# Cross attention: reciprocals in two halves over two steps, quotients in a third, output product two steps later

## Chip, cores and metric

The kernel runs on one core of a Trainium2 chip. The metric is the device time of one execution in microseconds (us); the median of three runs stands for a kernel.

## What is computed

The reference is a chain of six blocks on x (32 x 64 x 256): cross attention to ctx (32 x 1601 x 128), self attention, a layer of experts, a second cross attention to the same ctx, a state space block in two directions, and a feed forward block. The change is in the code of the cross attention, which the kernel calls twice (tags x0 and x1; the profile prints both as x). Cut to what matters:

```python
qh = (q @ Wq + bq).reshape(B, LQ, HEADS, D_K)      # q: layer norm of x, 32 x 64 x 256
kh = (k @ Wk + bk).reshape(B, LKV, HEADS, D_K)     # k = v = ctx, LKV = 1601, 16 heads of 16
vh = (v @ Wv + bv).reshape(B, LKV, HEADS, D_K)
scores = einsum('bhqd,bhkd->bhqk', qh, kh) * scale
attn = softmax(scores, axis=-1)
out = einsum('bhqk,bhkd->bhqd', attn, vh)
x = x + concat(out) @ Wo + bo
```

## The kernel before

One image (index b or u, 32 of them) is worked off in NG = 7 steps g = 0 to 6, each with two tiles of 128 keys (the last step has one, of 65). The loop over all steps s = 7u + g is unrolled, and each engine has its own list in program order; they meet at semaphores. In step s of image u there are:

- TensorE: `largest` (M, four products, L481: scores of image u + 1 for their maxima; two quads of heads ahead of the scores, two inside them), `scores` (L557, and L563, which subtracts the maximum), `project_keys` (K, L468: a seventh of a later image's keys), `project_values` (V, L499), in step 6 `turn_maxes` (T, L489: transposes of the negated maxima), then `weigh` (P, L531: probabilities times values of the step before). Step 1 adds `spread_sums` (S, L507), which spreads the softmax sums of the image before over the rows. `project_out` (W, L514) is the output product of two finished images, once in two images.
- VectorE: `keep_max` (L714, four reductions that read M), `keep_shift` in step 6 (L721 and L724), `gather` (L748 and L751: adds P's result to u_sb), `keep_sums` (L728) in step 1, `divide` (L733 reciprocal of the sums, L735 quotients oT = u_sb times reciprocal) and `add_out` (L740: adds W's result to x).
- ScalarE: the exponentials (L654), and copies of K and V out of their banks (L627, L635). GpSimd: kT_hi (L678), the queries (L663) and the split of the raw context into two parts (L367, L369). The queue of SP loads the raw context.

K's seven shares go over six stretches of 512 keys and a narrow one of 65 keys for both halves of the features; `key_share` hands the narrow share to K in step 4, and the maxima of the narrow share are M of step 6.

What ties the engines: M, K, V, T, P, S and W all write into misc_ps, a ring of NMB = 4 PSUM banks in the order of the list ORDER. An operation waits until the operation four places before it in ORDER has been read out (`open_bank`), by ScalarE for K and V and by VectorE for all others. The counts are worked out from the same list `step_ops`, so moving an operation there moves its place in the ring.

Around the change, VectorE in image u > 0 does in step 2: four maxima, `divide` of image u - 1 (both instructions), `gather`. In step 3 of even images TensorE ends the step with W, and VectorE with `add_out`. In the last image (u = 31) there are no maxima, K or V left, and after the loop the last S, divide and W stand alone.

Of the kernel before, what the change touches and what calls it, by code (L numbers as in the profile page):

```python
# [14 lines left out]
B, LQ, D = 32, 64, 256  # L15
# [246 lines left out]
def cross_attention(nc, tag, x_sb, ident, x_sel, pair_mask, ctxT, wq, wk, wv, wo, bq, bv, bo):  # L262
# [3 lines left out]
    GROUPS = 4  # L266
# [22 lines left out]
    def key_share(u, g):  # L289

        return (u + 1 + (g + 2) // NG, (g + 2) % NG)
# [4 lines left out]
    def step_ops(s):  # L296

        u, g = divmod(s, NG)
        ops = [("M", u + 1, g, j) for j in TRAIL + LEAD] if u + 1 < B else []
        if key_share(u, g)[0] < B:  # L300
            ops.append(("K",) + key_share(u, g))
        if s + 2 < STEPS:
            ops.append(("V", s + 2))
        if g == NG - 1 and u + 1 < B:
            ops.append(("T", u + 1))
        if s > 0:
            ops.append(("P", s - 1))
        if g == 1 and u > 0:
            ops.append(("S", u - 1))
        if g == 3 and u % 2 == 0 and u > 0:  # L310
            ops.append(("W", u // 2 - 1))
        return ops

# [9 lines left out]
    with ExitStack() as ctx:  # L323
# [77 lines left out]
        sums = sb(f"{tag}_sums", [P, GROUPS * LQ])  # L401
        recip = sb(f"{tag}_recip", [P, GROUPS * LQ])
# [15 lines left out]
        recip_done = sem(f"{tag}_recip_done")  # L418
# [14 lines left out]
        def read_out(e, op):  # L433

            reader, n = READ[AT[op]]
            e.wait_ge(act_free if reader == "act" else dve_free, n)
# [10 lines left out]
        def _(pe):  # L447
# [13 lines left out]
            def project_keys(op):  # L461
                _, b, n = op
                dst = open_bank(op)
                pe.wait_ge(raw_lo_done, split_of(b, SHARES[n][0][1]))
                for m, (c, k0, kn) in enumerate(SHARES[n]):
                    kn += kn % 2
                    for i, (w, part) in enumerate(((wk_hi, raw_hi), (wk_lo, raw_hi), (wk_hi, raw_lo))):
                        ins = nc.tensor.matmul(dst[:, m * kn:(m + 1) * kn], w[:, c * P:(c + 1) * P],  # L468
                                               part[:, b % 2, k0:k0 + kn], start=i == 0, stop=i == 2)
                ins.then_inc(misc_ready, 1)  # L470
# [14 lines left out]
            def turn_maxes(op):  # L485
                dst = open_bank(op)
                pe.wait_ge(max_done, op[1] + 1)
                for c in range(KD):
                    ins = nc.tensor.transpose(dst[:, c * P:(c + 1) * P],  # L489
                                              neg_max[:, c, :, :].rearrange("p j n -> p (j n)"), ident[:, :])  # L490
                ins.then_inc(misc_ready, 1)

            def project_values(op):
                b, g = divmod(op[1], NG)
                dst = open_bank(op)
                pe.wait_ge(raw_lo_done, split_of(b, tiles(g)[-1] * P))
                for h, i in enumerate(tiles(g)):
                    for m, (part, w) in enumerate(((raw_hi, wv_hi), (raw_hi, wv_lo), (raw_lo, wv_hi))):
                        ins = nc.tensor.matmul(dst[0:keys(i), h * D:(h + 1) * D], part[:, b % 2, cols(i)], w[:, :],  # L499
                                               start=m == 0, stop=m == 2)  # L500
                ins.then_inc(misc_ready, 1)
# [98 lines left out]
            for s in range(STEPS):  # L600
                u, g = divmod(s, NG)
                scores(s)
                if key_share(u, g)[0] < B:
                    project_keys(("K",) + key_share(u, g))
                if s + 2 < STEPS:
                    project_values(("V", s + 2))
                if g == NG - 1 and u + 1 < B:
                    turn_maxes(("T", u + 1))
                if s > 0:
                    weigh(("P", s - 1))  # L610
                if g == 1 and u > 0:
                    spread_sums(("S", u - 1))
                if g == 3 and u % 2 == 0 and u > 0:
                    project_out(("W", u // 2 - 1))
            weigh(("P", STEPS - 1))
            spread_sums(("S", B - 1))
# [89 lines left out]
        @block.vector  # L706
        def _(dve):
            def keep_max(op):
                _, b, n, j = op
                made(dve, op)  # L710
                c, k0, kn = SHARES[n][0]
                m = len(SHARES[n])
                even = kn + kn % 2
                nc.vector.tensor_reduce(maxes[:, c:c + m, j, k0 // NB],  # L714
                                        bank(op)[:, 0:m * even].rearrange("p (c k) -> p c k", c=m)[:, :, 0:kn],
                                        AX.X, ALU.max).then_inc(dve_free, 1)

            def keep_shift(op):
                b = op[1]
                read_out(dve, ORDER[max(n for n in range(AT[op]) if ORDER[n][0] == "M")])  # L720
                nc.vector.tensor_reduce(neg_max[:, :, :, 0], maxes[:, :, :, :], AX.X, ALU.max, negate=True  # L721
                                        ).then_inc(max_done, 1)
                made(dve, op)
                nc.vector.tensor_copy(shift[:, b % 2, :], bank(op)[:, 0:2 * P]).then_inc(dve_free, 1)  # L724

            def keep_sums(op):
                made(dve, op)
                nc.vector.tensor_copy(sums[:, :], bank(op)[:, 0:GROUPS * LQ]).then_inc(dve_free, 1)  # L728

            def divide(op):  # L730
                b = op[1]
                read_out(dve, op)
                nc.vector.reciprocal(recip[:, :], sums[:, :]).then_inc(recip_done, 1)  # L733
                dve.wait_ge(recip_done, b + 1)
                nc.vector.tensor_tensor(oT[:, :, b % 2, :], u_sb[:, b % 2, :, :],  # L735
                                        recip[:, :].rearrange("p (r q) -> p r q", q=LQ), ALU.mult).then_inc(o_done, 1)

            def add_out(op):
                made(dve, op)
                nc.vector.tensor_tensor(x_sb[:, op[1], :], bank(op)[:, 0:D], x_sb[:, op[1], :], ALU.add).then_inc(dve_free, 1)  # L740

            def gather(op):

                b, g = divmod(op[1], NG)
                total = u_sb[:, b % 2, :, :].rearrange("p r q -> p (r q)")
                made(dve, op)
                if g == 0:
                    nc.vector.tensor_copy(total, bank(op)[:, 0:GROUPS * LQ]).then_inc(dve_free, 1)  # L748
                else:
                    read_out(dve, ("P", op[1] - 1))  # L750
                    nc.vector.tensor_tensor(total, bank(op)[:, 0:GROUPS * LQ], total, ALU.add).then_inc(dve_free, 1)  # L751

            nc.vector.memset(ones[:, :].bitcast(F32), 1.0)
            nc.vector.memset(neg_max[:, :, :, :], 0.0)
            nc.vector.memset(oT[:, :, :, :], 0.0).then_inc(const_done, 1)
            dve.wait_ge(const_done, 1)
            if bo is not None:
                made(dve, ("C",))
                nc.vector.tensor_tensor(bias[:, :], bank(("C",))[:, 0:D], bo_sb[:, :], ALU.add).then_inc(dve_free, 1)
                read_out(dve, ("C",))  # L760
                nc.vector.tensor_tensor(x_sb, x_sb, bias[:, :].rearrange("p (a d) -> p a d", a=1).broadcast_to([P, NT, D]),
                                        ALU.add).then_inc(bias_done, 1)
                dve.wait_ge(bias_done, 1)
            for n in range(NG):
                for j in range(QUADS):
                    keep_max(("M", 0, n, j))
            keep_shift(("T", 0))
            for s in range(STEPS):
                u, g = divmod(s, NG)
                if u + 1 < B:  # L770
                    for j in TRAIL + LEAD:
                        keep_max(("M", u + 1, g, j))
                if g == 2 and u > 0:
                    divide(("S", u - 1))
                if g == NG - 1 and u + 1 < B:
                    keep_shift(("T", u + 1))
                if s > 0:
                    gather(("P", s - 1))
                if g == 1 and u > 0:
                    keep_sums(("S", u - 1))  # L780
                if g == 3 and u % 2 == 0 and u > 0:
                    add_out(("W", u // 2 - 1))
            gather(("P", STEPS - 1))
            keep_sums(("S", B - 1))
            divide(("S", B - 1))
            add_out(("W", B // 2 - 1))

# [1434 lines left out]
```

## Time and profile before

| | |
|---|---|
| median of three runs | 4064.31 us (4061.2 to 4066.16) |
| the profiled execution | 4061.75 us |
| its span on the core | 4059.8 us |
| first cross attention, main loop | about 92 to 1054 us of the span |
| second cross attention, main loop | about 1843 to 2790 us |
| TensorE busy | 3550.4 us, 87% |
| VectorE busy | 2756.5 us, 68% |
| ScalarE busy | 1951.2 us, 48% |
| GpSimd busy | 1562.0 us, 38% |

PE is TensorE, PEld its weight loads (which run beside the products), DVE VectorE, ACT ScalarE, POOL GpSimd. A row of a timeline gives the start and the duration in us, engine, line, operation, the tile written and the tiles read, the shape and the number of instructions merged; in brackets stands how long the engine had been idle before it, and what ended that. Ends of TensorE's products are modelled. The profile is of one execution; all durations below are from it.

### The profile page before, as it was taken

What the parts mean: (1) busy time and instruction counts of PE and PEld (TensorE: products, weight loads), DVE (VectorE), ACT (ScalarE), POOL (GpSimd) and SP (SyncE); (2) the same over time, 40 slices, a digit from 0 to 9 for tenths busy, and PEclk for the clock granted to TensorE, in tenths of its full rate; (3) what the DMA queues carried; (4) which work ended last, traced back from release to release, by engine and by line L of the source; (5) the groups of instructions that cost most, each with busy time, mean ns of one, the idle gap of its engine ahead of it and who ended that gap; (6) DMA issues with size and microseconds to landing.
All of it is one profiled execution on the core that took longest, in us unless ns stands there. A gap on an engine that the chain in (4) does not pass through costs nothing. (4 is left out here: it accounts for less than half of the span.)

```text
span 4059.8 us, 128360 instructions
## 1 busy us (share of the span) xinstructions
PE 3550.4 (87%) x53914; PEld 2521.8 (62%) x53915; DVE 2756.5 (68%) x4627; ACT 1951.2 (48%) x3015; POOL 1562.0 (38%) x1491
## 2 busy tenths in 40 slices
PE   6999999999783699669999999998788888877778
PEld 4888888888672466448888888885233333333357
DVE  5777777777543122257777777776799999999964
ACT  2666666666441122126666666664444444444432
POOL 3333333333132100233333333330088777778800
PEclk8999999999895899869999999998898989999889
DMA  2010010000006100110100010000132222222200
GB/s 67 28 36 28 28 34 29 28 28 20 10 1 244 46 31 31 49 56 28 36 28 28 30 33 28 28 20 25 24 81 71 72 70 68 70 72 81 72 25 21
DMA packets 79948, 182.69 MB, mean 45 GB/s; under 512 B 10754, under 2 KB 31266, under 8 KB 79042
## 3 DMA queue, kind: packets, MB, share of 16 engines
q1 hardware_dynamic: 76354, 166.57, 13.2%
q8 instruction: 421, 6.90, 0.7%
q0 software_dynamic: 3072, 8.39, 0.6%
q14 instruction: 101, 0.83, 0.1%
HBM read 157.36 MB, written 17.56 MB: 43 GB/s over the span
## 5 line engine op out<-in xcount | busy, mean ns | idle before, releaser
L654 ACT ACTIVATE x_probs<-x_score_ps 128x1024 f32<-128x1024 f32 (+1 forms) x896 | 814.2, 960 | 708.2 <-PE x_score_ps L563 701.9
L714 DVE TENSOR_REDUCE x_maxes<-x_misc_ps 128x1 f32<-128x512 f32 (+1 forms) x1792 | 1020.9, 625 | 31.0 <-PE x_misc_ps L481 25.6
L678 POOL CAST x_kT_hi<-x_kT 128x512 fp32r<-128x512 f32 (+1 forms) x448 | 256.3, 572 | 1286.5 <-ACT x_kT L627 1063.1
L1742 PE MATMUL b_acc_ps<-b_read,ident 128*128 128x512 f32 x1024 | 571.1, 689 | 183.5 <-POOL b_read L1828 150.3
L1820 POOL TENSOR_TENSOR b_drive<-b_b_all,b_dtx 128x1024 f32<-128x1024 f32 x256 | 602.6, 2355 | 332.8 <-DVE b_dtx L1900 282.0
L1862 DVE TENSOR_TENSOR_SCAN b_state<-b_decay_ps,b_drive 128x512 f32<-128x512 f32 x512 | 607.0, 1205 | 12.5 <-POOL b_drive L1820 12.5
L557 PE MATMUL x_score_ps<-x_qz,x_kT 32*128 32x128 f32 x13312 | 591.2, 277 | 1.4 <-issue 1.2
L1810 ACT ACTIVATE b_decay_ps<-b_dt,b_a_neg 128x504 f32<-128x504 f32 x512 | 350.0, 685 | 462.3 <-DVE b_state L1862 462.3
L1742 PEld LDWEIGHTS b_acc_ps<-b_read,ident 128*128 128x128 f32 x1024 | 196.1, 213 | 503.8 <-POOL b_read L1828 251.1
L557 PEld LDWEIGHTS x_score_ps<-x_qz,x_kT 32*128 32x128 f32 x13312 | 501.4, 182 | 4.5 <-issue 2.5
L531 PE MATMUL x_misc_ps<-x_probs,x_v 128*32 128x64 f32 x26624 | 464.5, 221 | 0.0
L481 PE MATMUL x_misc_ps<-x_kT_hi,x_qz_hi 32*128 32x512 f32 (+1 forms) x2048 | 451.0, 410 | 11.8 <-POOL x_kT_hi L678 3.0
L531 PEld LDWEIGHTS x_misc_ps<-x_probs,x_v 128*32 128x32 f32 x26624 | 392.2, 110 | 65.7 <-issue 23.2
L751 DVE TENSOR_TENSOR x_u<-x_misc_ps,x_u 128x256 f32<-128x256 f32 x384 | 162.1, 422 | 324.0 <-PE x_misc_ps L531 324.0
L563 PE MATMUL x_score_ps<-x_shift,x_ones 1*128 1x512 f32 (+1 forms) x1792 | 327.5, 458 | 1.2 <-issue 1.1
L627 ACT ACTIVATE x_kT<-x_misc_ps 128x512 f32<-128x512 f32 (+1 forms) x448 | 250.2, 558 | 86.7 <-PE x_misc_ps L468 86.7
L481 PEld LDWEIGHTS x_misc_ps<-x_kT_hi,x_qz_hi 32*128 32x128 f32 x2048 | 219.6, 186 | 114.0 <-DVE x_u L751 31.2
L635 ACT ACTIVATE x_v<-x_misc_ps 128x512 f32<-128x512 f32 (+1 forms) x448 | 259.2, 578 | 24.0 <-PE x_misc_ps L499 11.8
L1872 DVE TENSOR_TENSOR b_read<-b_c_ps,b_state 128x512 f32<-128x512 f32 x384 | 254.0, 662 | 0.3 <-DVE b_state L1862 0.3
L468 PE MATMUL x_misc_ps<-x_raw_hi,x_wk_hi 128*128 128x512 f32 (+1 forms) x512 | 232.9, 455 | 15.8 <-POOL x_v L684 8.9
L369 POOL TENSOR_TENSOR x_raw_lo<-x_raw,x_raw_hi 128x512 fp32r<-128x512 f32 (+1 forms) x192 | 235.7, 1228 | 15.6
L499 PE MATMUL x_misc_ps<-x_wv_hi,x_raw_hi 128*128 128x256 f32 (+1 forms) x832 | 237.8, 286 | 0.0
(283 smaller groups left out, 5607.9 us busy)
## 6 DMA issues: line engine op xcount, KB each, us to landing
x_raw<-in_ctxT SPq DMA_DIRECT2D x64, 800.5 KB, 4.5
b_b_all<-b_bc_rows SPq DMA_DIRECT2D x128, 256.0 KB, 3.6
b_c_all<-b_bc_rows SPq DMA_DIRECT2D x128, 256.0 KB, 3.1
m_w<-in_m_w SPq DMA_DIRECT2D x16, 704.0 KB, 19.3
m_w<-in_m_w SPq DMA_DIRECT2D x8, 768.0 KB, 20.3
m_slot_rows<-m_zero SPq DMA_DIRECT2D x1, 4992.0 KB, 17.2
m_block_rows<-m_slot_rows SPq DMA_DIRECT2D x39, 128.0 KB, 2.0
m_slot_out<-m_out SPq DMA_DIRECT2D x39, 128.0 KB, 1.7
```

The lines of the kernel that those rows point to most:

```text
L481: ins = nc.tensor.matmul(dst[:, m * kn:(m + 1) * kn], qz_hi[rows, b % 2, c, :, :].rearrange("p s q -> p (s q)"), kT_hi[rows, (b * NG + n) ...
L531: ins = nc.tensor.matmul(dst[j * 32:(j + 1) * 32, r * LQ:(r + 1) * LQ], v_sb[0:keys(i), g, h, 8 * c + 2 * j + half, :], probs[0:keys(i), s ...
L557: nc.tensor.matmul(score_ps[0:kn, j, n * P:(n + 1) * P], kT[rows, u % 2, c, cols(mine[h])], qz[rows, u % 2, c, :, :].rearrange("p s q -> p ...
L563: nc.tensor.matmul(score_ps[0:kn, j, 0:len(mine) * 2 * P], ones[j * 32:j * 32 + 1, 0:kn], shift[j * 32:j * 32 + 1, u % 2, :].rearrange("p ...
L635: nc.scalar.activation(v_sb[rows, g, 0:n, :, 0:DH].rearrange("p a h d -> p (a h) d"), bank(op)[rows, 0:n * D].rearrange("p (a d) -> p a d" ...
L654: nc.scalar.activation(probs[rows, s % 2, js, 0:n], score_ps[rows, js, 0:n], ACT.Exp).then_inc(exp_done, 1)
L678: nc.gpsimd.tensor_copy(kT_hi[:, at % 3, 0:m * even].rearrange("p (c k) -> p c k", c=m)[:, :, 0:kn], kT[:, b % 2, c:c + m, k0:k0 + kn]).th ...
L714: nc.vector.tensor_reduce(maxes[:, c:c + m, j, k0 // NB], bank(op)[:, 0:m * even].rearrange("p (c k) -> p c k", c=m)[:, :, 0:kn], AX.X, AL ...
L1742: nc.tensor.matmul(acc_ps[:, c, :], ident[:, :], read[:, c, :], start=False, stop=True, skip_group_check=True).then_inc(acc_done, 1)
L1810: nc.scalar.activation(by_sequence(decay_ps[:, c % 2, :])[:, :, inside(p)], by_sequence(dt[:, c, :])[:, :, inside(p)], ACT.Exp, scale=a_ne ...
L1820: nc.gpsimd.tensor_tensor(drive[:, c:c + 2, :], b_all[:, k % 2:k % 2 + 1, :].broadcast_to([P, 2, NB]), dtx[:, c:c + 2, :], ALU.mult).then_ ...
L1862: nc.vector.tensor_tensor_scan(order(state[:, c, :]), order(decay_ps[:, c % 2, :]), order(drive[:, c, :]), 0.0, ALU.mult, ALU.add).then_in ...
```

## The change

`divide` becomes two functions. `invert(op, half)` takes the reciprocal of 128 of the 256 columns of the sums; it runs in step 2 for the first half and in step 3 for the second. `divide` now only makes the quotients, in step 4. `project_out` and `add_out` move from step 3 to step 5 of even images, in `step_ops`, in TensorE's loop and in VectorE's. Behind the loop both halves, the quotients and the last W follow each other as before.

```diff
--- before.py
+++ after.py
@@ -307,7 +307,7 @@
             ops.append(("P", s - 1))
         if g == 1 and u > 0:
             ops.append(("S", u - 1))
-        if g == 3 and u % 2 == 0 and u > 0:
+        if g == 5 and u % 2 == 0 and u > 0:
             ops.append(("W", u // 2 - 1))
         return ops
 
@@ -610,7 +610,7 @@
                     weigh(("P", s - 1))
                 if g == 1 and u > 0:
                     spread_sums(("S", u - 1))
-                if g == 3 and u % 2 == 0 and u > 0:
+                if g == 5 and u % 2 == 0 and u > 0:
                     project_out(("W", u // 2 - 1))
             weigh(("P", STEPS - 1))
             spread_sums(("S", B - 1))
@@ -727,11 +727,16 @@
                 made(dve, op)
                 nc.vector.tensor_copy(sums[:, :], bank(op)[:, 0:GROUPS * LQ]).then_inc(dve_free, 1)
 
+            HALF = GROUPS * LQ // 2
+
+            def invert(op, half):
+                read_out(dve, op)
+                of = slice(half * HALF, (half + 1) * HALF)
+                nc.vector.reciprocal(recip[:, of], sums[:, of]).then_inc(recip_done, 1)
+
             def divide(op):
                 b = op[1]
-                read_out(dve, op)
-                nc.vector.reciprocal(recip[:, :], sums[:, :]).then_inc(recip_done, 1)
-                dve.wait_ge(recip_done, b + 1)
+                dve.wait_ge(recip_done, 2 * b + 2)
                 nc.vector.tensor_tensor(oT[:, :, b % 2, :], u_sb[:, b % 2, :, :],
                                         recip[:, :].rearrange("p (r q) -> p r q", q=LQ), ALU.mult).then_inc(o_done, 1)
 
@@ -770,7 +775,9 @@
                 if u + 1 < B:
                     for j in TRAIL + LEAD:
                         keep_max(("M", u + 1, g, j))
-                if g == 2 and u > 0:
+                if g in (2, 3) and u > 0:
+                    invert(("S", u - 1), g - 2)
+                if g == 4 and u > 0:
                     divide(("S", u - 1))
                 if g == NG - 1 and u + 1 < B:
                     keep_shift(("T", u + 1))
@@ -778,10 +785,12 @@
                     gather(("P", s - 1))
                 if g == 1 and u > 0:
                     keep_sums(("S", u - 1))
-                if g == 3 and u % 2 == 0 and u > 0:
+                if g == 5 and u % 2 == 0 and u > 0:
                     add_out(("W", u // 2 - 1))
             gather(("P", STEPS - 1))
             keep_sums(("S", B - 1))
+            for half in range(2):
+                invert(("S", B - 1), half)
             divide(("S", B - 1))
             add_out(("W", B // 2 - 1))
```

VectorE's list, from the copy of the sums in step 1 of an even image to the maxima of step 4. Before (L728 the sums, L714 four maxima, L733 reciprocal, L735 quotients, L751 gather, L740 add_out):

```order
L728 COPY x_sums<-x_misc_ps 128x256
L714 TENSOR_REDUCE x_maxes<-x_misc_ps 128x1 x4
L733 RECIPROCAL x_recip<-x_sums 128x256
L735 TENSOR_TENSOR x_oT<-x_u,x_recip 128x4x64
L751 TENSOR_TENSOR x_u<-x_misc_ps,x_u 128x256
L714 TENSOR_REDUCE x_maxes<-x_misc_ps 128x1 x4
L751 TENSOR_TENSOR x_u<-x_misc_ps,x_u 128x256
L740 TENSOR_TENSOR x<-x_misc_ps,x 128x256
L714 TENSOR_REDUCE x_maxes<-x_misc_ps 128x1 x4
```

The same stretch now, on to step 6 (L735 is now the reciprocal, L740 the quotients, L756 the gather, L745 add_out):

```order
L728 COPY x_sums<-x_misc_ps 128x256
L714 TENSOR_REDUCE x_maxes<-x_misc_ps 128x1 x4
L735 RECIPROCAL x_recip<-x_sums 128x128
L756 TENSOR_TENSOR x_u<-x_misc_ps,x_u 128x256
L714 TENSOR_REDUCE x_maxes<-x_misc_ps 128x1 x4
L735 RECIPROCAL x_recip<-x_sums 128x128
L756 TENSOR_TENSOR x_u<-x_misc_ps,x_u 128x256
L714 TENSOR_REDUCE x_maxes<-x_misc_ps 128x1 x4
L740 TENSOR_TENSOR x_oT<-x_u,x_recip 128x4x64
L756 TENSOR_TENSOR x_u<-x_misc_ps,x_u 128x256
L714 TENSOR_REDUCE x_maxes<-x_misc_ps 128x1 x4
L756 TENSOR_TENSOR x_u<-x_misc_ps,x_u 128x256
```

Between the maxima and the gather of step 2 stood two instructions of full width; now one of half width stands there in step 2, one in step 3, and the quotients in step 4.

TensorE's list at the first place where W moves, the difference of the two (L531 the value products, L514 W, L481 the maxima of the next step, narrow in the second piece):

```order
@@ -359,5 +359,4 @@
 L499 MATMUL x0_misc_ps<-x0_wv_hi,x0_raw_lo 128x256
 L531 MATMUL x0_misc_ps<-x0_probs,x0_v 32x64 x32
-L514 MATMUL x0_misc_ps<-x0_wo,x0_oT 128x256 x4
 L481 MATMUL x0_misc_ps<-x0_kT_hi,x0_qz_hi 128x512 x2
 L557 MATMUL x0_score_ps<-x0_qz,x0_kT 128x128 x14
@@ -392,4 +391,5 @@
 L499 MATMUL x0_misc_ps<-x0_wv_hi,x0_raw_lo 128x256
 L531 MATMUL x0_misc_ps<-x0_probs,x0_v 32x64 x32
+L514 MATMUL x0_misc_ps<-x0_wo,x0_oT 128x256 x4
 L481 MATMUL x0_misc_ps<-x0_kT_hi,x0_qz_hi 128x66 x4
 L557 MATMUL x0_score_ps<-x0_qz,x0_kT 65x128 x6
```

W stood between step 3 and the wide step 4; it stands now between step 5 and the narrow step 6.

## Rows read from the trace of the kernel before

**Rows 1.** The page, busy us of each engine, share of the span, instructions.

```profile
PE 3550.4 (87%) x53914; PEld 2521.8 (62%) x53915; DVE 2756.5 (68%) x4627; ACT 1951.2 (48%) x3015; POOL 1562.0 (38%) x1491
```

**Rows 2.** Busy time in a stretch: length, PE, PEld, DVE, ACT, POOL, TensorE's granted clock, DMA share, GB/s.

```profile
200.00:500.00 300.00, 296.93 (x7317) 246.12 (x7306) 216.22 (x393) 187.18 (x273) 100.97 (x144) 1.00 0.10 31
```

**Rows 3.** Who waited for whom, 100 to 1060 us: us in total, times, longest.

```profile
...
PEld x_misc_ps L468 <- DVE x_maxes L714: 16.9, 48, 0.4
PEld x_misc_ps L481 <- DVE x_u L751: 15.7, 29, 0.6
...
```

**Rows 4.** Timeline of TensorE, steps 2 to 4 of an odd image.

```profile
...
496.24 1.10 PE L531 MATMUL x_misc_ps<-x_probs,x_v 128*32 128x64 f32 x64
...
499.61 0.50 PE L468 MATMUL x_misc_ps<-x_raw_hi,x_wk_hi 128*128 128x512 f32 x1
...
501.20 1.10 PE L531 MATMUL x_misc_ps<-x_probs,x_v 128*32 128x64 f32 x64
...
503.79 0.30 PE L468 MATMUL x_misc_ps<-x_raw_hi,x_wk_hi 128*128 128x66 f32 x1
...
```

**Rows 5.** Timeline of VectorE, the same steps.

```profile
...
493.60 2.48 DVE L714 TENSOR_REDUCE x_maxes<-x_misc_ps 128x1 f32<-128x512 f32 x4
496.00 1.74 DVE L733 RECIPROCAL x_recip<-x_sums 128x256 f32<-128x256 f32 x1
497.78 0.84 DVE L735 TENSOR_TENSOR x_oT<-x_u,x_recip 128x256 f32<-128x256 f32 x1
498.54 0.41 DVE L751 TENSOR_TENSOR x_u<-x_misc_ps,x_u 128x256 f32<-128x256 f32 x1
...
502.37 0.42 DVE L751 TENSOR_TENSOR x_u<-x_misc_ps,x_u 128x256 f32<-128x256 f32 x1 [1.03 <-PE x_misc_ps L531]
502.77 2.48 DVE L714 TENSOR_REDUCE x_maxes<-x_misc_ps 128x1 f32<-128x512 f32 x4
506.13 0.42 DVE L751 TENSOR_TENSOR x_u<-x_misc_ps,x_u 128x256 f32<-128x256 f32 x1 [0.87 <-PE x_misc_ps L531]
...
```

**Rows 6.** Timelines of TensorE and VectorE, steps 3 to 6 of an even image.

```profile
...
532.05 1.99 PE L514 MATMUL x_misc_ps<-x_wo,x_oT 128*128 128x256 f32 x8
...
536.70 1.10 PE L531 MATMUL x_misc_ps<-x_probs,x_v 128*32 128x64 f32 x64
...
540.90 1.10 PE L531 MATMUL x_misc_ps<-x_probs,x_v 128*32 128x64 f32 x64
...
544.40 0.38 PE L489 MATMUL x_misc_ps<-ident,x_neg_max 128*128 128x128 f32 x2
...
```

```profile
...
534.08 0.42 DVE L740 TENSOR_TENSOR x<-x_misc_ps,x 128x256 f32<-128x256 f32 x1 [1.47 <-PE x_misc_ps L514]
...
542.07 0.42 DVE L751 TENSOR_TENSOR x_u<-x_misc_ps,x_u 128x256 f32<-128x256 f32 x1 [1.32 <-PE x_misc_ps L531]
...
543.42 0.19 DVE L721 TENSOR_REDUCE x_neg_max<-x_maxes 128x8 f32<-128x32 f32 x1
544.82 0.42 DVE L724 CAST x_shift<-x_misc_ps 128x256 fp32r<-128x256 f32 x1 [1.21 <-PE x_misc_ps L489]
...
```

**Rows 7.** Timelines of TensorE and VectorE, steps 2 and 3 of image u = 30.

```profile
...
1018.72 1.10 PE L531 MATMUL x_misc_ps<-x_probs,x_v 128*32 128x64 f32 x64
...
1020.29 0.42 DVE L735 TENSOR_TENSOR x_oT<-x_u,x_recip 128x256 f32<-128x256 f32 x1
...
1023.29 1.10 PE L531 MATMUL x_misc_ps<-x_probs,x_v 128*32 128x64 f32 x64
...
```

**Rows 8.** Groups by line: total busy us, mean ns of one, idle before.

```profile
...
L733 DVE RECIPROCAL x_recip<-x_sums 128x256 f32<-128x256 f32 x64 | 111.5, 1742 | 0.1
...
L1021 DVE RECIPROCAL s_recip<-s_sums 128x16 f32<-128x16 f32 x16 | 4.0, 253 | 0.6
...
```

**Rows 9.** Timeline of GpSimd, steps 2 to 4 of the odd image of rows 4.

```profile
...
497.72 0.61 POOL L663 TENSOR_TENSOR x_qz_hi<-x_qT,x_mask 128x256 fp32r<-128x256 f32 x1
...
506.00 0.29 POOL L678 CAST x_kT_hi<-x_kT 128x130 fp32r<-128x130 f32 x1 [2.30 <-ACT x_kT L627]
...
```

## The prediction

> **What bounds the kernel now.** I read the page's busy row first: TensorE is busy 87% of the span, VectorE 68%, ScalarE 48% [rows 1]. The busy time by stretch sharpens this for the code in question: in 300 us inside the first attention TensorE works 297 us at the full granted clock (1.00, that is 2.4 GHz), VectorE 216 us [rows 2]. So an attention lasts as long as TensorE's list of work, plus the few places where TensorE stops. A shorter VectorE list is worth nothing by itself; only what removes a stop of TensorE counts.
>
> The view of who waited for whom gives the stops [rows 3]. In the first attention TensorE's loads sit idle 29 times, 15.7 us in all, before the maxima's matmuls (L481) until VectorE's gather (L751), and 16.9 us before the key projection (L468) until a maximum (L714). 29 is nearly the number of images in which VectorE divides while the next image's maxima are computed: u = 1 to 30. So once an image something on VectorE is late.
>
> The timelines show it [rows 4, 5]. In the image at 490 us, step g = 2 ends with the value products (L531) at 496.24 + 1.10 = 497.34. The gather that empties their bank should follow 0.07 us later, as it does in the next step (502.30, gather at 502.37). It starts at 498.54, since VectorE has done four maxima (to 496.08), then the reciprocal (1.74) and the quotients (0.84). In the next step the second leading maximum needs that bank: banks go round in fours. It, the first maximum behind the gather and then the keys wait in turn: the key projection starts at 499.61. Two distances follow.
> - Undisturbed, the keys start 1.49 us after the products' end (503.79 - 502.30).
> - After a late gather they start 1.07 us after its start (499.61 - 498.54).
>
> So a gather may start 0.42 us behind the products' end and cost nothing. Beyond that TensorE pays all of it: 498.54 + 1.07 - 497.34 - 1.49 = 0.78 us. The interval between the products' starts says the same: 501.20 - 496.24 = 4.96 in step 3, against 540.90 - 536.70 = 4.20 in step 5, which has the same tiles and no divide [rows 4, 6]. I take 0.77.
>
> A check comes with the trace. The quotients take 0.84 us in most images, but 0.42 in u = 30. There the interval is 1023.29 - 1018.72 = 4.57, and the stop 0.37: 0.41 less for 0.42 us less on VectorE [rows 7]. The cost is one to one.
>
> **What the change does to this stop.** The reciprocal of 128x256 takes 1742 ns, that of 128x16 elsewhere in the kernel 253 ns [rows 8]. That is (1742 - 253)/240 = 6.2 ns a column, and 253 + 112 x 6.2 = 947 ns for 128x128. Two halves take 1.89 us, 0.15 more than the whole. Bounds for a half: 0.87 (no fixed part) and 1.74 (width has no effect); the line between two measured widths lies close to the first. Now step by step, with what hides each piece.
> - Step 2: the maxima end at 496.08 and the gather is due at 497.41, a gap of 1.33 us. A half with 0.04 us of gap before the next instruction ends at 497.07. Slack 0.34, and another 0.35 before TensorE notices. The stop of 0.77 goes.
> - Step 3: the gather now starts at 497.41, four maxima end 0.40 + 2.48 later at 500.29, and the products, undisturbed, end at 497.34 + 4.20 = 501.54. The second half ends at 501.28, 0.33 before the gather's turn at 501.61.
> - Step 4: the narrow key share makes this the short one. The maxima end at 505.25 and the gather is due at 506.13: 0.88 us [rows 5]. The quotients fit if they take 0.84 and with room at 0.42. If they were late by 0.1, step 5 is a wide step and forgives 0.35. Cost 0.
> - What is late next: after that no step of the image has VectorE work besides its own. TensorE then runs step 3 like step 5, which shows that neither ScalarE nor GpSimd nor a DMA holds a wide step above 4.20. The raw context tiles come on SP's queue, which is moved past nothing.
>
> How long will the quotients be? GpSimd's row says why they take 0.84: in step 2 its products for qz_hi start at 497.72 and run 0.61 us, under the quotients at 497.78. In u = 30 there is no such product beside them, and they take 0.42. In step 4 GpSimd sits idle for 2.30 us up to 506.00, just when the quotients run (505.3 to 505.7) [rows 5, 7, 9]. So I take 0.42. The Trainium skill has the rule (SBUF — State Buffer, "Who interferes with whom"): a VectorE instruction with two SBUF inputs contends with a GpSimd instruction that reads SBUF, and the later one waits. The trace agrees here, with 0.84 beside such a product and 0.42 without it. By that rule the quotients shrink; by the flat reading they stay at 0.84; both fit the gap, so the sum is the same.
>
> The output product W (four products in eight passes, 1.99 us) moves from behind step 3 to behind step 5 of every even image, 30 times inside the loop. Its price on TensorE stays, since it waits for quotients that are a whole step old. New is what stands behind it: step 6, the narrow one, where fewer scores stand ahead of the second leading maximum, so that it asks sooner for the bank that add_out empties. add_out starts 0.04 us after W's end (534.08 against 534.04) and takes 0.42 [rows 6]. The gather does the same job for the narrow step today: starts at 542.07, 0.07 after the products' end, takes 0.42, and no row of the waits puts a stop of the narrow step on it: the 29 are the divides. add_out is even 0.03 nearer to its products' end. So I put W's cost there at 0; as its bound I allow a tenth of a us, 30 x 0.1 = 3 us, inside the range.
>
> Behind W on VectorE stand add_out, four narrow maxima (542.49 to 543.42: 0.93) and the negated maximum of all (0.19), and the transposes T need these. Today T starts at 544.40, 0.79 us after the negated maximum is done at 543.61; the distance to the step's start stays the same with W ahead. Cost 0.
>
> Last image: there are no maxima, nothing waits, and reciprocal, quotients and W stand in a row at the end of each attention. Two halves cost 2 x 0.15 = 0.3 us more.
>
> Sum: 58 images x 0.77 = 44.7, two images (u = 30) x 0.37 = 0.7, less 0.3 for the tails: 45.1 us saved. The profiled execution took 4061.75 us (span 4059.8), 2.6 below the median of 4064.31. I take the gain off the median: 4064.3 - 45.1 = 4019.2; off the profiled run it is 4016.7.
>
> **Rivals.**
> 1. Only part comes back (4026 to 4045). Something makes the gather late by more than 0.42 us again, in step 2, 3 or 4. A half would have to take over 0.95 + 0.34 + 0.35 = 1.64 us for that, so only the upper bound (1.74) would do it, and then by 0.1. Or a wait that today lies under the stop shows, say 0.3 us of ScalarE or GpSimd in 60 steps: 18 us, 4037. For it speaks that the step's key projection waits for a maximum 48 times, more often than there are divides [rows 3]; against it that step 5 has the same tiles and takes 4.20.
> 2. It does not do what it says (4060 to 4068): the stop belongs to the maxima's matmuls or to ScalarE, and the reciprocal only lies beside it. The image u = 30, where less VectorE time gave less stop one to one, speaks against it.
> 3. Slower, by W ahead of the narrow step. The mechanism: add_out, four narrow maxima, the negated maximum and the copy of T's result (0.42 + 0.93 + 0.19 + 0.42 = 1.96 us) stand behind W on VectorE. If none of it were covered, 30 x 1.96 = 59 us are lost against 45 won: 4078. It decides from 45/30 = 1.5 us a W. Against it: 0.79 us of slack before T and an even spacing today.
> 4. VectorE's list as the bound, with the fixed part of a reciprocal paid twice. If the attention were as long as that list, 62 x 0.15 = 9.3 us would come on top: 4074, less what shorter quotients give back. It decides only where VectorE has no idle time in a step; it is busy for 216 of 300 us [rows 2], so it is not so. The Trainium skill speaks against small pieces (VectorE: DVE Perf Modes, the section on the TRN2 errata): each instruction pays a latency of its own, so a large tile is better than many small ones. The trace agrees that there is a fixed part.
>
> **How the numbers follow.** The forecast, all of the stop gone, has 0.84; rival 1 has 0.08, rival 2 0.03, rivals 3 and 4 together 0.03, and a gain above the forecast's range 0.02. The forecast's own scatter: single runs of before differ by 5 us (4061.2 to 4066.2), and a new build may lay its instructions otherwise; I allow 7 us to either side. That makes 4012 to 4027; to bring in rival 1's near half I extend the upper end to 4031. A measurement here tells 0.2% (8 us) from no change; so faster 0.95, same 0.02, slower 0.03.
>
> **What would show it.** In the profile after: the L481 row waiting for the gather and the L468 row waiting for maxima (15.7 and 16.9 us) shrink, the first to near nothing; the interval from step 2's to step 3's products goes from 4.96 to 4.20; the halves take 0.95; the quotients 0.42; W's row stays at 1.99, with no new wait of L481 for add_out. Wrong would be: an interval in step 3 above 4.3, a late gather in step 4, or T starting later after W. A half above 1.64 us would bring the stop back.

## The result

| | before | changed |
|---|---|---|
| median | 4063.06 us (4 runs, 4061.2 to 4066.16) | 4011.8 us (4 runs, 4010.0 to 4014.43) |
| span of the profiled execution | 4059.8 us | 4008.4 us |

The ratio is 0.9874, 95% interval [0.9856, 0.9891]: 51 us or 1.3% faster. Forecast were 4019 us and a gain of 45 us, between 4012 and 4031. The time lies 0.2 us below that range, and the gain is 6 us larger than forecast. A second comparison of the same two kernels, made with the experiments, gave 4013.2 us for the changed one, inside the range.

TensorE's timeline in an odd image of the changed kernel, steps 2 to 4, answers to [rows 4]:

```profile
...
485.59 1.10 PE L531 MATMUL x_misc_ps<-x_probs,x_v 128*32 128x64 f32 x64
...
488.19 0.50 PE L468 MATMUL x_misc_ps<-x_raw_hi,x_wk_hi 128*128 128x512 f32 x1
...
489.78 1.10 PE L531 MATMUL x_misc_ps<-x_probs,x_v 128*32 128x64 f32 x64
...
493.55 1.10 PE L531 MATMUL x_misc_ps<-x_probs,x_v 128*32 128x64 f32 x64
...
```

The products of step 3 start 489.78 - 485.59 = 4.19 us after those of step 2; it was 4.96. The keys start 488.19 - 486.69 = 1.50 us after the products' end, undisturbed.

VectorE's timeline in the same image answers to [rows 5] (L735 is the reciprocal, L740 the quotients, L756 the gather):

```profile
...
482.99 2.48 DVE L714 TENSOR_REDUCE x_maxes<-x_misc_ps 128x1 f32<-128x512 f32 x4
485.39 0.94 DVE L735 RECIPROCAL x_recip<-x_sums 128x128 f32<-128x128 f32 x1
486.76 0.42 DVE L756 TENSOR_TENSOR x_u<-x_misc_ps,x_u 128x256 f32<-128x256 f32 x1 [0.43 <-PE x_misc_ps L531]
487.18 2.48 DVE L714 TENSOR_REDUCE x_maxes<-x_misc_ps 128x1 f32<-128x512 f32 x4
489.58 0.94 DVE L735 RECIPROCAL x_recip<-x_sums 128x128 f32<-128x128 f32 x1
490.95 0.42 DVE L756 TENSOR_TENSOR x_u<-x_misc_ps,x_u 128x256 f32<-128x256 f32 x1 [0.43 <-PE x_misc_ps L531]
491.37 2.48 DVE L714 TENSOR_REDUCE x_maxes<-x_misc_ps 128x1 f32<-128x512 f32 x4
493.77 0.41 DVE L740 TENSOR_TENSOR x_oT<-x_u,x_recip 128x256 f32<-128x256 f32 x1
494.72 0.42 DVE L756 TENSOR_TENSOR x_u<-x_misc_ps,x_u 128x256 f32<-128x256 f32 x1 [0.53 <-PE x_misc_ps L531]
...
```

Each gather has idle time before it, 0.43 to 0.53 us, that ends with the products: VectorE waits for TensorE again in each of these steps. A half takes 0.94 us, the quotients 0.41.

Who waited for whom in the first attention of the changed kernel, against [rows 3]:

```profile
...
PEld x_misc_ps L481 <- ACT x_v L635: 9.3, 28, 0.3
...
PEld x_misc_ps L468 <- DVE x_maxes L714: 3.5, 14, 0.3
...
```

The row of L481 waiting for the gather (15.7 us) is gone, that of L468 waiting for the maxima went from 16.9 to 3.5 us. Only the first of the two is a measure of the stop. Idle time of L468's loads for which the view names no releaser (its rows "issue") rose from 33.3 to 41.6 us at the same time, so that L468 lost 5.1 us in all; and quot_step3 below keeps 8.9 us of L468 waiting for maxima without any stop. The row of L481 waiting for the values' copy (L635) is 9.3 us in both kernels.

**Where the 51 us are.** Two groups mark the ends of each attention: the exponentials (L654) and add_out (L740 before, L745 now), with their first and last start. Before, then changed:

```profile
L654 ACT ACTIVATE x_probs<-x_score_ps x448: 582/1021/1029, 86.7 to 1058.5; 128x1024 f32<-128x1024 f32 x128, 65x512 f32<-65x512 f32 x22
L740 DVE TENSOR_TENSOR x<-x_misc_ps,x x16: 423/425/425, 162.5 to 1067.5; 128x256 f32<-128x256 f32 x16
L654 ACT ACTIVATE x_probs<-x_score_ps x448: 581/1021/1029, 1813.5 to 2784.6; 128x1024 f32<-128x1024 f32 x128, 65x512 f32<-65x512 f32 x22
L740 DVE TENSOR_TENSOR x<-x_misc_ps,x x16: 424/424/426, 1890.2 to 2793.3; 128x256 f32<-128x256 f32 x16
```

```profile
L654 ACT ACTIVATE x_probs<-x_score_ps x448: 582/1021/1030, 86.9 to 1032.9; 128x1024 f32<-128x1024 f32 x128, 65x512 f32<-65x512 f32 x22
L745 DVE TENSOR_TENSOR x<-x_misc_ps,x x16: 423/424/425, 169.1 to 1042.2; 128x256 f32<-128x256 f32 x16
L654 ACT ACTIVATE x_probs<-x_score_ps x448: 582/1021/1031, 1783.4 to 2733.9; 128x1024 f32<-128x1024 f32 x128, 65x512 f32<-65x512 f32 x22
L745 DVE TENSOR_TENSOR x<-x_misc_ps,x x16: 423/425/425, 1869.1 to 2742.5; 128x256 f32<-128x256 f32 x16
```

The first attention takes 980.8 us before and 955.3 now, the second 979.8 and 959.1: 46.2 us together, where 45.1 were forecast. The two do not gain alike, 25.5 and 20.7 us; in a second pair of traces (after_again and before_again below) it is 23.5 and 22.9, so one attention alone scatters more than the two together. The stretch between them (self attention, experts and the second attention's start, code that the change doesn't touch) takes 746.0 and 741.2 us: 4.8 us. What is left, 0.4 us, lies ahead and behind. So the attentions did what was forecast, and most of the surplus comes from untouched code. The experiments ask two things: which part of the change brings the 46 us, and whether the 5 us belong to the change.

### The profile page after: what moved, and what is told of

Read it like the earlier page. It is cut to its first block and busy times, and to the rows that moved or that the text cites. A ratio compares the mean times of both kernels' runs of the same rounds, so it can differ in the third digit from the quotient of the medians.

```text
span 4008.4 us, 128424 instructions
## 1 busy us (share of the span) xinstructions
PE 3504.0 (87%) x53914; PEld 2508.5 (63%) x53915; DVE 2740.8 (68%) x4691; ACT 1943.7 (48%) x3015; POOL 1561.9 (39%) x1491
## 5 line engine op out<-in xcount | busy, mean ns | idle before, releaser
L654 ACT ACTIVATE x_probs<-x_score_ps 128x1024 f32<-128x1024 f32 (+1 forms) x896 | 814.2, 961 | 673.8 <-PE x_score_ps L563 667.3
L714 DVE TENSOR_REDUCE x_maxes<-x_misc_ps 128x1 f32<-128x512 f32 (+1 forms) x1792 | 1021.9, 627 | 29.3 <-PE x_misc_ps L481 23.0
L678 POOL CAST x_kT_hi<-x_kT 128x512 fp32r<-128x512 f32 (+1 forms) x448 | 256.9, 574 | 1235.6 <-ACT x_kT L627 1119.5
L531 PE MATMUL x_misc_ps<-x_probs,x_v 128*32 128x64 f32 x26624 | 464.5, 221 | 0.0
L531 PEld LDWEIGHTS x_misc_ps<-x_probs,x_v 128*32 128x32 f32 x26624 | 392.5, 110 | 65.5 <-issue 23.3
L481 PE MATMUL x_misc_ps<-x_kT_hi,x_qz_hi 32*128 32x512 f32 (+1 forms) x2048 | 422.2, 406 | 5.5 <-POOL x_kT_hi L678 4.1
L756 DVE TENSOR_TENSOR x_u<-x_misc_ps,x_u 128x256 f32<-128x256 f32 x384 | 162.9, 424 | 295.9 <-PE x_misc_ps L531 295.9
L563 PE MATMUL x_score_ps<-x_shift,x_ones 1*128 1x512 f32 (+1 forms) x1792 | 310.7, 456 | 1.1 <-issue 1.1
L635 ACT ACTIVATE x_v<-x_misc_ps 128x512 f32<-128x512 f32 (+1 forms) x448 | 260.3, 581 | 18.9 <-PE x_misc_ps L499 12.5
L481 PEld LDWEIGHTS x_misc_ps<-x_kT_hi,x_qz_hi 32*128 32x128 f32 x2048 | 207.9, 186 | 81.9 <-ACT x_v L635 18.9
L468 PE MATMUL x_misc_ps<-x_raw_hi,x_wk_hi 128*128 128x512 f32 (+1 forms) x512 | 232.1, 453 | 11.2 <-POOL x_v L684 8.9
```

Of the source, the lines that this page charges most:

```text
L481: ins = nc.tensor.matmul(dst[:, m * kn:(m + 1) * kn], qz_hi[rows, b % 2, c, :, :].rearrange("p s q -> p (s q)"), kT_hi[rows, (b * NG + n) ...
L531: ins = nc.tensor.matmul(dst[j * 32:(j + 1) * 32, r * LQ:(r + 1) * LQ], v_sb[0:keys(i), g, h, 8 * c + 2 * j + half, :], probs[0:keys(i), s ...
L563: nc.tensor.matmul(score_ps[0:kn, j, 0:len(mine) * 2 * P], ones[j * 32:j * 32 + 1, 0:kn], shift[j * 32:j * 32 + 1, u % 2, :].rearrange("p ...
L635: nc.scalar.activation(v_sb[rows, g, 0:n, :, 0:DH].rearrange("p a h d -> p (a h) d"), bank(op)[rows, 0:n * D].rearrange("p (a d) -> p a d" ...
L654: nc.scalar.activation(probs[rows, s % 2, js, 0:n], score_ps[rows, js, 0:n], ACT.Exp).then_inc(exp_done, 1)
L678: nc.gpsimd.tensor_copy(kT_hi[:, at % 3, 0:m * even].rearrange("p (c k) -> p c k", c=m)[:, :, 0:kn], kT[:, b % 2, c:c + m, k0:k0 + kn]).th ...
```

## The experiments

All kernels have the same four marks; the attentions' two lengths are added up as "attentions", the stretch between them is "between". Step 3 and the images are measured between the starts of the value products, as medians; the length of an image adds up its steps' medians and is good to about 0.03 us. Single images can be longer.

| kernel | span us | attentions us | between us | step 3, odd image (median) | whole odd / even image |
|---|---|---|---|---|---|
| before | 4059.8 | 1960.6 | 746.0 | 4.98 | 29.73 / 31.67 |
| changed | 4008.4 | 1914.4 | 741.2 | 4.19 | 28.97 / 30.82 |
| w_only | 4058.2 | 1962.3 | 744.3 | 4.97 | 29.73 / 31.63 |
| quot_step3 | 4018.0 | 1916.4 | 747.4 | 4.19 | 28.97 / 30.84 |
| halves_quot_step3 | 4027.1 | 1924.1 | 749.6 | 4.19 | 28.97 / 31.11 |
| w_step4 | 4023.6 | 1914.0 | 752.7 | 4.19 | 28.97 / 30.88 |
| after_again | 4010.2 | 1913.0 | 744.3 | 4.19 | 28.97 / 30.81 |
| before_again | 4061.7 | 1959.4 | 749.6 | 4.97 | 29.73 / 31.66 |
| dose1 | 4010.9 | 1914.6 | 744.3 | 4.19 | 28.97 / 30.81 |
| dose2 | 4050.1 | 1954.6 | 744.3 | 4.89 | 29.65 / 31.52 |

### w_only: the output product's move alone

```diff
-        if g == 3 and u % 2 == 0 and u > 0:
+        if g == 5 and u % 2 == 0 and u > 0:
```

(in the order list, in TensorE's loop and in VectorE's; `divide` stays whole in step 2.)

> Before, with the output product and add_out moved from step 3 to step 5 and nothing else. Theory (the stop is the late gather of step 2): it stays, the interval of the value products in step 3 is 4.96 to 4.98 us, and the time is that of before within 3 us. Rival (the move of W brings part of the gain: even images gained 0.85 us an image against 0.76 in odd ones): even images take 0.08 us less, 30 x 0.08 = 2.4 us. Rival (W ahead of the narrow step costs): slower by up to 3 us, with waits of L481 for add_out.

Measured: 4062.04 us against 4062.84, ratio 0.9996 [0.9987, 1.0005]. The stop is there unchanged: 4.97 us in step 3, and TensorE's loads wait for the gather as before.

```profile
...
PEld x_misc_ps L481 <- DVE x_u L751: 15.6, 29, 0.6
PEld x_misc_ps L468 <- DVE x_maxes L714: 15.0, 41, 0.4
...
```

An even image takes 31.63 us instead of 31.67. So W's place is worth at most some 0.04 us of the 0.85 that an even image gains, about 1 us in all and hardly more than these medians resolve, and the narrow step behind W costs nothing. The rival in which that place costs is out as well: no row of L481 waits for add_out (L740).

### quot_step3: the quotients one step later, nothing else

```diff
-            def divide(op):
-                b = op[1]
+            def invert(op):
                 read_out(dve, op)
                 nc.vector.reciprocal(recip[:, :], sums[:, :]).then_inc(recip_done, 1)
+
+            def divide(op):
+                b = op[1]
                 dve.wait_ge(recip_done, b + 1)
...
                 if g == 2 and u > 0:
+                    invert(("S", u - 1))
+                if g == 3 and u > 0:
                     divide(("S", u - 1))
```

> Before, with the whole reciprocal in step 2 and only the quotients one step later; W stays in step 3. Threshold theory: the gather of step 2 starts 1.74 + 0.04 - 1.33 = 0.45 us after its turn, of which 0.35 is forgiven, so a stop of 0.10 us is left, 60 x 0.10 = 6 us above the changed kernel, near 4018 us (39 us below before, less what the clock does outside). Rival (the halves matter, any late gather costs in full): a stop of 0.45, 27 us above the changed kernel, 4039 us. Rival (the quotients alone were the whole cost): 4012 us.

Measured: 4017.98 us, ratio 0.9883 [0.9868, 0.9898]. That is the threshold theory's number, but its mechanism is not what the trace shows. Step 3 takes 4.19 us: no stop is left at all. That the time came out at 4018 is luck. The attentions are 2.0 us longer than the changed kernel's, about 1 us of which may be W's place (w_only); of the other 7.6 us between the two profiled spans 6.2 are the stretch between the attentions (747.4 against 741.2 us), and the rest lies behind them. VectorE's timeline, step 2 (L732 is the reciprocal, L753 the gather, L737 the quotients):

```profile
...
482.38 2.48 DVE L714 TENSOR_REDUCE x_maxes<-x_misc_ps 128x1 f32<-128x512 f32 x4
484.78 1.74 DVE L732 RECIPROCAL x_recip<-x_sums 128x256 f32<-128x256 f32 x1
486.44 0.36 DVE L753 TENSOR_TENSOR x_u<-x_misc_ps,x_u 128x256 f32<-128x256 f32 x1
486.72 2.47 DVE L714 TENSOR_REDUCE x_maxes<-x_misc_ps 128x1 f32<-128x512 f32 x4
489.10 0.42 DVE L737 TENSOR_TENSOR x_oT<-x_u,x_recip 128x256 f32<-128x256 f32 x1
...
```

The gather is late, but by 0.29 us and not by 0.45. In the changed kernel it follows 486.76 - 482.99 = 3.77 us after the start of the maxima; here it starts 4.06 us after. My sum took the maxima's end by their row and added a gap of 0.04 before the gather; instructions that stand ready start up to 0.08 us ahead of their predecessor's end in these rows (486.44 against 486.52). 0.29 lies inside what is forgiven, so nothing stops. The quotients take 0.42 us in step 3 too, with no GpSimd instruction beside them. So the whole reciprocal could have stayed: **moving the quotients out of step 2 brings the gain, the halves bring nothing on top that the trace would show.** By the times alone a few us for the halves can't be excluded: w_step4, which has them and ran in the same comparison, took 4015.14 us (4011.2 to 4025.6) against 4017.98 (4015.0 to 4019.9).

### halves_quot_step3: halves, quotients behind the second, W left in step 3

```diff
-                if g == 4 and u > 0:
+                if g == 3 and u > 0:
                     divide(("S", u - 1))
...
-                if g == 5 and u % 2 == 0 and u > 0:
+                if g == 3 and u % 2 == 0 and u > 0:
```

(against the changed kernel.)

> Halves in steps 2 and 3, the quotients in step 3 behind the second half, W in step 3 as before. Step 3 then has 0.94 + 0.42 to 0.84 us on VectorE in a gap of 1.32. With quotients of 0.42 the gather is late by 0.1 and nothing stops: 4012 us. With 0.84 (GpSimd splits the context in that step) it is late by 0.5, 0.35 forgiven: 0.15 x 60 = 9 us more, 4021 us. Rival (quotients must be two steps ahead of W): W waits in even images, over 4025 us.

Measured: 4022.66 us, ratio 0.9894 [0.9879, 0.9909]. Odd images are as fast as in the changed kernel (28.97), even ones 0.29 us slower. The timelines of an even image, VectorE and then TensorE:

```profile
...
518.81 0.94 DVE L735 RECIPROCAL x_recip<-x_sums 128x128 f32<-128x128 f32 x1
519.79 0.42 DVE L740 TENSOR_TENSOR x_oT<-x_u,x_recip 128x256 f32<-128x256 f32 x1
520.20 0.42 DVE L756 TENSOR_TENSOR x_u<-x_misc_ps,x_u 128x256 f32<-128x256 f32 x1
...
```

```profile
...
520.36 1.97 PE L514 MATMUL x_misc_ps<-x_wo,x_oT 128*128 128x256 f32 x8 [0.23 <-DVE x_oT L740]
...
```

The quotients do take 0.42 (once 0.54 among 64), so the gather is only a little late and forgiven. But W at the end of this step needs them at 520.21, and waits 0.23 us, in 30 images: 7 to 9 us. That was in neither of my first two cases; the rival about W had the place right and the size too large. Once the second half delays the quotients, W must go later: that is what W's move pays for. In 57 of the 64 places GpSimd's cast of the keys (L678) starts about 0.18 us after these quotients. Here it is the cast that gets longer, 0.72 us (median); beside gathers, maxima and reciprocals a cast of this width keeps its 0.61. In the kernel before, where GpSimd's product (L663) started 0.06 us ahead of the quotients, it was the quotients that doubled. In both kernels the one that started second took longer.

### w_step4: W behind step 4

```diff
-                if g == 5 and u % 2 == 0 and u > 0:
+                if g == 4 and u % 2 == 0 and u > 0:
```

> The changed kernel with W and add_out behind step 4 in place of step 5. Theory (W costs its 1.9 us wherever it stands): 4012 us within 2.5 us. Rival (W ahead of the narrow step is a little dearer or cheaper than ahead of a wide one): even images differ by 0.03 to 0.1 us from 30.82, 1 to 3 us in all. Were the quotients not ready at the end of step 4, a wait of L514 would show.

Measured: 4015.14 us median, ratio 0.9875 [0.986, 0.989]; the attentions take 1914.0 us against 1914.4. The median lies 3.1 us above the forecast of 4012, a little outside its 2.5 us. Even images take 30.88 instead of 30.82, 0.06 us, 2 us in all, and no wait of L514 shows inside the loop. W costs 1.9 us wherever it stands: of an even image, the step that follows it takes 5.68 us when W stands behind step 3, 6.12 behind step 4 and 5.69 behind step 5; the same steps take 3.76, 4.18 and 3.80 us without it. The profiled execution has a span of 4023.6 us although its attentions are as short as any: 752.7 us lie between them.

### after_again and before_again: the two kernels once more

> The changed kernel once more, for the 6 us that the forecast lacks. The step intervals should repeat to 0.02 us (28.97 and 30.82 an image). Theory (the rest is the scatter of the granted clock outside the changed code): the stretch between the two attentions, 741.2 us in the first trace of it and 744 to 753 in the five others, comes out anew, and the median of the time lies between 4010 and 4018. Rival (the new build runs these stages faster by itself): 741 us again and 4011 to 4012.

> The kernel before once more, for the same question: intervals of 4.96 to 4.98 in step 3 as in its first trace; the stretch between the attentions was 746.0 us and its self attention had 3 iterations of 11.1 us among 15 of 7.9. By the theory of a scattering clock these numbers change from run to run; by the rival they repeat.

Measured: the changed kernel 4013.2 us (4008.01 to 4018.16) beside 4060.32 us for before, ratio 0.9889 [0.9871, 0.9907], or 45 us (the two medians differ by 47). The attentions repeat within 1.4 us in both kernels (1914.4 and 1913.0; 1960.6 and 1959.4). The stretch between them does not: 741.2 and 744.3 us, 746.0 and 749.6. It is the same program in each pair, so this is scatter from run to run. Nor does it follow the change over all ten traces: it is 744.3 to 749.6 us in the three with `divide` whole in step 2, 741.2 to 752.7 in the seven others. So the first expectation's theory holds: the stretch came out anew and the median lies between 4010 and 4018. By its rival the 741 us would have come again.

What scatters is TensorE's clock. The stretch has the same 2934 products in before and in the changed kernel, VectorE is busy 228.3 and 228.6 us of it, but TensorE 541.8 and 537.0: 4.8 us, the whole difference, at a granted clock of 0.82 and 0.83 on average. In the longest, w_step4, TensorE is busy 548.4 us for as many products, at 0.81.

A part of it can be located. In self attention 16 iterations follow each other, seen in GpSimd's fold of the probabilities. Most are 7.9 us apart, some 11.1. Busy time of one iteration of either kind, changed kernel (columns as in [rows 2]):

```profile
1096.90:1104.60 7.70, 6.67 (x77) 5.97 (x76) 3.87 (x8) 3.65 (x8) 3.06 (x4) 1.00 0.01 2
1128.40:1139.40 11.00, 9.97 (x88) 9.21 (x88) 3.90 (x9) 3.65 (x8) 3.07 (x4) 0.81 0.00 0
```

VectorE, ScalarE and GpSimd do the same in both; the second lasts 3.3 us longer, at a granted clock of 0.81 instead of 1.00: for a while TensorE runs at the lower of its two levels (1.2 and 2.4 GHz). The counts of products differ (77 and 88), as the cut takes in more of the next iteration's projection. Like with like, the 16 products of one projection (L900), at full clock and in the slow stretch:

```profile
...
1095.63 2.00 PE L900 MATMUL s_qk_ps<-s_xnT,s_w 128*128 128x128 f32 x16
...
1128.48 3.73 PE L900 MATMUL s_qk_ps<-s_xnT,s_w 128*128 128x128 f32 x16
...
```

These alone lose 1.7 of the 3.3 us. Before had three such long iterations, the changed kernel two, and three in its second trace, which is 3.1 us longer here; w_step4, with the longest stretch between, had four. One of them fewer is 3.3 of the 4.8 us. What sets them off was not tried.

### dose1 and dose2: one and two more reciprocals in step 2

```diff
+            def again(times):
+                for n in range(times):
+                    nc.vector.reciprocal(spare[:, n * HALF:(n + 1) * HALF], sums[:, 0:HALF])
...
                     invert(("S", u - 1), g - 2)
+                    if g == 2:
+                        again(2)
```

(against the changed kernel; dose1 has `again(1)`. `spare` is a tile of its own that nobody reads, so they only add work.)

> The changed kernel with one more reciprocal of 128x128 behind the first half in step 2 (into a tile that nobody reads): a known dose of 0.89 to 0.94 us. The gap in step 2 has 0.43 us left, so the gather starts 0.46 to 0.51 us late. With 0.35 forgiven: a stop of 0.11 to 0.16 us, 60 times, 7 to 10 us: 4019 to 4022. Rival (all lateness costs): 0.5 x 60 = 30 us, 4042. Rival (no stop until later): 4012.

> Two more such reciprocals in step 2. By the first theory the whole second dose of 0.89 us lands on TensorE: a stop of 1.0 to 1.05 us, 60 to 63 us, 4072 to 4075, slower than before, whose VectorE list in step 2 is 0.2 us shorter. If a VectorE delay were absorbed elsewhere (by the idle time of later steps), it would be less than 0.8 us a dose.

Measured: dose1 4014.93 us (ratio 0.9896 [0.9880, 0.9913]), dose2 4057.91 us (0.9999 [0.9989, 1.0008]). In the trace of dose1 the gather is 0.30 us late and step 3 takes 4.19: no stop, where 0.11 to 0.16 us were expected. The trace of dose2, VectorE (L736 and L740 are the reciprocals, L761 the gather), then TensorE (L532 are the value products, L469 the keys):

```profile
...
490.22 2.48 DVE L715 TENSOR_REDUCE x_maxes<-x_misc_ps 128x1 f32<-128x512 f32 x4
492.62 0.94 DVE L736 RECIPROCAL x_recip<-x_sums 128x128 f32<-128x128 f32 x1
493.48 1.71 DVE L740 RECIPROCAL x_spare<-x_sums 128x128 f32<-128x128 f32 x2
495.11 0.36 DVE L761 TENSOR_TENSOR x_u<-x_misc_ps,x_u 128x256 f32<-128x256 f32 x1
...
```

```profile
...
492.87 1.10 PE L532 MATMUL x_misc_ps<-x_probs,x_v 128*32 128x64 f32 x64
...
496.11 0.50 PE L469 MATMUL x_misc_ps<-x_raw_hi,x_wk_hi 128*128 128x512 f32 x1
...
497.73 1.10 PE L532 MATMUL x_misc_ps<-x_probs,x_v 128*32 128x64 f32 x64
...
```

The gather comes 1.14 us behind the products' end (493.97), and the keys start 1.00 us after it, 2.14 behind that end; undisturbed they start 1.50 behind it. So 0.64 us of stop, and 497.73 - 492.87 = 4.86 for the step. The three reciprocals take 495.11 - 492.62 = 2.49 us together, not the 0.94 + 2 x 0.89 = 2.72 that I had laid out, and what is forgiven is 1.50 - 1.00 = 0.50 us behind the products' end, not 0.42. Both errors shrink the stop from the expected 1.0 us to 0.64 in this image, 0.70 in the median. TensorE's waits name the gather again: L482 (the maxima's products here) waits 30 times for it, 13.1 us in the first attention, where the changed kernel has no such row. dose1 adds 0.2 us to the attentions, dose2 adds 40.2 (1954.6 - 1914.4).

What this shows of the threshold: a gather 0.29 or 0.30 us late costs nothing (quot_step3, dose1), one 1.1 us late costs 0.7 to 0.8 (dose2, before), and one 0.74 us late costs 0.37 (before, u = 30). Between 0.74 and 1.14 us the cost is one to one. The threshold itself, 0.35 to 0.43 us beyond the gather's turn, is worked out and was not tried from both sides.

## The prediction, point by point

- **What bounds it.** Right. It was a stop of TensorE, once an image, caused by VectorE's divide. With the quotients out of step 2 the stop is gone (quot_step3), with VectorE work put back it returns (dose2), and with W alone moved it stays (w_only).
- **Size of the stop, 0.77 us.** Odd images gained 29.73 - 28.97 = 0.76. Even images gained 31.67 - 30.82 = 0.85: their step 3 went from 4.98 to 4.18 (0.80), and W's new place gives 0.04. I had read the undisturbed step off once, at 4.20. By these usual images the gain would be about 47 us; single longer images took some of it back (the 15 odd ones of the changed kernel add up to 435.7 us in the first attention and 439.1 in the second). The marks give 46.2 and, in the second pair of traces, 46.4 against the 45.1 forecast. The sum was 1 us short, no more than the 1.4 by which the attentions of one kernel repeat.
- **The halves.** The line between two widths gave 0.947, measured 0.942. Their use was misread: by my own sum the whole reciprocal without the quotients would have been late by 0.45 us against 0.35 forgiven. It is late by 0.29, so one edit of the three would do, within the few us that the times leave open.
- **The quotients at 0.42 us.** Right: 410 to 425 ns in all 64, and no GpSimd instruction overlaps any of them. No time hung on it, since by the sum 0.84 fits the gap of step 4 as well. The Trainium skill (SBUF — State Buffer, "Who interferes with whom") says that a VectorE instruction with two SBUF inputs contends with a GpSimd instruction that reads SBUF. The traces agree: 0.84 us beside GpSimd's product before, 0.41 alone now.
- **W ahead of the narrow step, cost 0.** Right, from the even image of the changed kernel (TensorE):

```profile
...
527.69 2.00 PE L514 MATMUL x_misc_ps<-x_wo,x_oT 128*128 128x256 f32 x8
529.61 0.30 PE L481 MATMUL x_misc_ps<-x_kT_hi,x_qz_hi 32*128 32x66 f32 x2
...
532.03 0.38 PE L489 MATMUL x_misc_ps<-ident,x_neg_max 128*128 128x128 f32 x2
...
```

and VectorE:

```profile
...
529.72 0.42 DVE L745 TENSOR_TENSOR x<-x_misc_ps,x 128x256 f32<-128x256 f32 x1 [1.47 <-PE x_misc_ps L514]
530.06 1.00 DVE L714 TENSOR_REDUCE x_maxes<-x_misc_ps 128x2 f32<-128x130 f32 x4
531.10 0.19 DVE L721 TENSOR_REDUCE x_neg_max<-x_maxes 128x8 f32<-128x32 f32 x1
...
```

  T starts 532.03 - 531.29 = 0.74 us after the negated maximum; it was 0.79 [rows 6]. Rival 3 had no ground.
- **The tails, 0.3 us dearer.** Not seen: back to back the two halves take 1.77 us, hardly more than the whole (1.74 to 1.75). So the fixed 0.15 us of a reciprocal, which this term and rival 4 counted for each half, is nearly hidden where two follow each other. 0.3 us too much in the sum.
- **The step that failed.** Not the mechanism, but the level that the gain was taken off and the scatter around it.
  - "I take the gain off the median: 4064.3 - 45.1 = 4019.2." That median is of three runs. A fourth brought it to 4063.06, and the 32 runs of before made beside all comparisons have a median of 4061.9: the start was 1.2 to 2.4 us too high. The other number in that sentence's paragraph, 4016.7 off the profiled run, would have put 4011.8 inside the same 7 us.
  - "I allow 7 us to either side." It rests on the same three runs, which differ by 5 us, and the sum has no term for the code outside the attentions. The 32 runs go from 4054.1 to 4070.1 us, 16 us apart, and the untouched stretch between the attentions alone from 741.2 to 752.7 over ten traces.

  The 7.4 us from 4019.2 to 4011.8 are then, roughly: 1.2 us of start, 1.1 us in the attentions, 4.8 us in the stretch between them and 0.4 us ahead and behind. That it ended 0.2 us outside and not inside is chance: the second comparison's median, 4013.2, is inside, and the median of all eight runs of the changed kernel is 4012.7. Its 45 us by the ratio, 47 by the medians, stand beside 46.4 in the attentions of its traces. So the mechanism and its size stand.

## What to carry to other kernels

Look for the place where the bound engine's idle time names the same helper once per round, and measure there how late the helper may be before it costs: here 0.3 us beyond its turn were free, and of 1.1 us all but about 0.4 was paid. Move the smallest piece that brings the lateness under that threshold, since a further split adds work and may pull other steps (here W) with it. Before calling one per cent a gain, or drawing a range around it, compare the stretches of code that did not change.

## What the runs showed that I had not expected

- Instructions that stand ready on VectorE follow each other faster than their rows add up: reciprocals of 0.94 us start 0.86 and about 0.81 us apart, and a late gather right behind a reciprocal takes 0.36 us instead of 0.42 (quot_step3, dose1, dose2), so that late work catches up a little. Behind the quotients it does not: 0.41 to 0.42 (before, halves_quot_step3).
- In self attention TensorE's clock falls for a while in two to four of 16 iterations, a different number in two executions of the same program; each costs 3.3 us.
- When VectorE's quotients and a GpSimd instruction overlap, the one that starts second is the one that takes longer: the quotients 0.84 us instead of 0.41 in before, GpSimd's cast 0.72 instead of 0.61 in halves_quot_step3.
